# A two-layer graph kernel on one core: 13 adjacency tiles per chunk, four PSUM banks for the late chains, 41 split tiles, and a first tile in four pieces

## The chip, the cores and the metric

The kernel runs on one core of a Trainium2 chip. The metric is device time in microseconds, lower is better. Times of the profile are counted from the start of its span.

## The reference

```python
N = 8192                      # nodes; 128 channels
h = maximum(layernorm(x), 0)
r = where((adj < 0.5) & ~eye, adj, 1.0)
S = where((adj < 0.5) & ~eye, exp(-(1/r - 1/mu)**2 / (2*sigma**2)), 0)
x = x + S @ (h @ W0 + B0)                 # layer 0
h = maximum(layernorm(x), 0)
x = x + (adj*adj + eye) @ (h @ W1.T)      # layer 1
```

`adj` is 8192x8192 in fp32, 256 MB. Layer 0 needs a nonlinear function of each element, layer 1 its square.

## The kernel before

Everything is transposed: channels on partitions. `adj` is cut into 16x16 blocks of 512x512; a block is one tile of 128x2048 fp32 (1 MB, four groups of 128 columns of `adj`). Row block c of layer 0 ("chunk c", steps 16c to 16c+15) takes 16 S tiles. Step s masks S tile s; `square(s-2)` and `sensitivity(s-2)` run two steps behind, and TensorE multiplies S tile s-3 in step s.

**An S tile** passes through five instructions: VectorE `premask` (cutoff, L604), ScalarE `log` (L778), ScalarE `reciprocal` (L783), VectorE `square` (L611), ScalarE `sensitivity` (L788); then TensorE's `l1` (L434, four fp32 matmuls, eight records) into `p_l1a` or `p_l1b`. A diagonal block first gets 1 added to its diagonal (`add_eye`, L589), which the cutoff then masks out.

**An adj tile** of layer 1 is an `Item` (row, source): it is squared in place by VectorE (`square_adj`, L622) or ScalarE (L796), a diagonal one gets the eye added, and TensorE multiplies it with the second layer's features of the source block (L468). The features of a source block exist only once its chunk of layer 0 is done (`add_x1` L677, `relu_row` L684, `keep_h2` L691 on VectorE, `centre_row` L503 on TensorE, and so on). `make_plan` therefore fills chunk c with tiles whose source is known: `QUOTA[c]` tiles, and the rest comes in the last chunk (steps 240 to 255, "dense") and behind it (the "tail", one tile per step). Most tiles of a row form a `Chain`: consecutive tiles that sum in one PSUM bank. At the chain's end VectorE copies the bank to `xa_buf` (`add_chain`, L718), and GpSimd's queue adds the buffer onto the output in DRAM (L893). In steady chunks the chains use banks `p_x0` and `p_x1`; before, only the last 16 chains, those of the tail, use four (also `p_own0` and `p_l1a`).

**A split tile** is written as two fp32r tiles, `high` (a CAST, L639) and `low` (the difference, L641), by `halves` on VectorE; TensorE then makes three matmuls per group (L446 to L448, twelve records) in place of a group's two fp32 records. There are three `high` buffers, so `halves` of split tile n waits for TensorE to have used split tile n-3. On VectorE the halves of item m stand behind the squaring of item m+1.

All engines run their instructions in the order written. The loads of both kinds of tiles share a ring of 8 buffers (`A_RING`), S tiles one of 7, of which the dense chunk uses three: `premask(t)` there waits for `s_used`, TensorE's end of S tile t-3. `EVAC` is the number of items after a chain's last one at which VectorE copies its bank. SP's queue issues all loads in order.

## Time and profile before

| | us |
|---|---|
| median of 3 runs | 1880.04 |
| lowest, highest | 1878.95, 1880.99 |
| the profiled execution | 1879.75 |
| its span | 1877.9 |
| TensorE busy | 1840.0 |
| VectorE busy | 1723.2 |
| ScalarE busy | 1730.2 |

The busy times are sums of records, and a matmul's record lasts longer than the distance to the next one, so they hide gaps. The distance between two starts on an engine is called its pitch below. A chunk is measured from one `centre_row` to the next.

### The profile page before, as it was taken

What the parts mean: (1) busy time and instruction counts of PE and PEld (TensorE: products, weight loads), DVE (VectorE), ACT (ScalarE), POOL (GpSimd) and SP (SyncE); (2) the same over time, 40 slices, a digit from 0 to 9 for tenths busy, and PEclk for the clock granted to TensorE, in tenths of its full rate; (3) what the DMA queues carried; (4) which work ended last, traced back from release to release, by engine and by line L of the source; (5) the groups of instructions that cost most, each with busy time, mean ns of one, the idle gap of its engine ahead of it and who ended that gap; (6) DMA issues with size and microseconds to landing.
All of it is one profiled execution on the core that took longest, in us unless ns stands there. A gap on an engine that the chain in (4) does not pass through costs nothing.

```text
span 1877.9 us, 13284 instructions
## 1 busy us (share of the span) xinstructions
PE 1840.0 (98%) x4820; PEld 879.6 (47%) x4820; DVE 1723.2 (92%) x1012; ACT 1730.2 (92%) x986; POOL 87.6 (5%) x110
## 2 busy tenths in 40 slices
PE   7999999999999999999999999999999999999998
PEld 4544444444444444444444444444444444555565
DVE  7999999999999999999999999999999955678686
ACT  8999999999999999999999999999999997777562
POOL 0000000000000000000000000000000000000011
PEclk9999999999999999999999999999999999999999
DMA  8476878987878787777677776666666578667997
GB/s 312 163 292 260 326 281 305 323 294 285 307 269 324 235 297 258 251 275 257 245 253 266 258 286 239 242 219 229 220 227 218 191 265 287 248 251 259 309 353 226
DMA packets 83138, 497.85 MB, mean 265 GB/s; under 512 B 9601, under 2 KB 10241, under 8 KB 26881
## 3 DMA queue, kind: packets, MB, share of 16 engines
q1 hardware_dynamic: 68832, 469.33, 65.4%
q0 software_dynamic: 14096, 27.53, 8.4%
q8 instruction: 39, 0.64, 0.1%
q14 instruction: 27, 0.21, 0.0%
q10 hardware_dynamic: 144, 0.13, 0.0%
HBM read 469.17 MB, written 27.79 MB: 265 GB/s over the span
## 4 chain that ended last, share of the span: by engine, by line
PE 43%; ACT 32%; DVE 18%; issue 6%; DMA 1%; SPq 0%; DVEq 0%; ACTq 0%
PE p_x L468 12%; PE p_l1b L434 11%; ACT rings L778 10%; ACT rings L783 9%; ACT rings L788 9%; PE p_l1a L434 8%; PE p_own L468 7%; DVE rings L611 6%; DVE rings L604 6%; DVE rings L622 3%; ACT rings L796 2%; PE p_x L446 1%; PE p_x L448 1%; PE p_x L447 1%; DVE high L639 1%
## 5 line engine op out<-in xcount | busy, mean ns | idle before, releaser
L611 DVE SCALAR_TENSOR_TENSOR rings<-rings,small 128x2048 f32<-128x2048 f32 x256 | 600.5, 2346 | 29.0 <-ACT rings L783 28.8
L604 DVE SCALAR_TENSOR_TENSOR rings<-rings 128x2048 f32<-128x2048 f32 x256 | 585.1, 2286 | 8.2 <-PE p_l1b L434 6.8
L788 ACT ACTIVATE rings<-rings,small 128x2048 f32<-128x2048 f32 x256 | 533.0, 2082 | 34.3 <-DVE rings L611 33.9
L778 ACT ACTIVATE rings<-rings,small 128x2048 f32<-128x2048 f32 x256 | 509.4, 1990 | 9.3 <-DVE rings L604 6.8
L468 PE MATMUL p_x<-rings,h 128*128 128x512 f32 x1128 | 505.4, 592 | 0.0
L783 ACT ACTIVATE rings<-rings 128x2048 f32<-128x2048 f32 x256 | 488.0, 1906 | 5.5
L434 PE MATMUL p_l1b<-rings,h 128*128 128x512 f32 x1024 | 460.9, 596 | 3.6 <-ACT rings L788 3.5
L434 PE MATMUL p_l1a<-rings,h 128*128 128x512 f32 x1024 | 459.5, 595 | 0.2
L468 PEld LDWEIGHTS p_x<-rings,h 128*128 128x128 f32 x1128 | 213.5, 190 | 261.1 <-issue 260.0
L622 DVE TENSOR_TENSOR rings<-rings 128x2048 f32<-128x2048 f32 x135 | 308.5, 2285 | 7.3 <-DMA rings<-adjT 4.6
L434 PEld LDWEIGHTS p_l1b<-rings,h 128*128 128x128 f32 x1024 | 194.3, 191 | 245.4 <-issue 236.9
L434 PEld LDWEIGHTS p_l1a<-rings,h 128*128 128x128 f32 x1024 | 193.6, 191 | 237.1 <-issue 234.2
L796 ACT ACTIVATE rings<-rings 128x2048 f32<-128x2048 f32 x121 | 226.7, 1900 | 59.5 <-DMA rings<-adjT 31.3
L468 PE MATMUL p_own<-rings,h 128*128 128x512 f32 x600 | 269.7, 592 | 0.0
L468 PEld LDWEIGHTS p_own<-rings,h 128*128 128x128 f32 x600 | 113.6, 190 | 138.0 <-issue 137.3
L893 POOL DMA_DIRECT2D outT<-xa_buf x89 | 74.2, 834 | 1502.6 <-DVE xa_buf L718 1455.3
L718 DVE COPY xa_buf<-p_x 128x512 f32<-128x512 f32 x82 | 56.1, 684 | 57.6 <-PE p_x L468 48.0
L641 DVE TENSOR_TENSOR low<-rings,high 128x2048 fp32r<-128x2048 f32 x37 | 84.8, 2293 | 1.3
L639 DVE CAST high<-rings 128x2048 fp32r<-128x2048 f32 x37 | 45.2, 1222 | 13.4 <-ACT rings L796 13.3
L446 PE MATMUL p_x<-high,h_high 128*128 128x512 f32 x108 | 49.2, 456 | 5.4 <-DVE low L641 5.4
L448 PE MATMUL p_x<-high,h_low 128*128 128x512 f32 x108 | 42.2, 391 | 0.0
L447 PE MATMUL p_x<-low,h_high 128*128 128x512 f32 x108 | 42.2, 390 | 0.0
(92 smaller groups left out, 498.9 us busy)
## 6 DMA issues: line engine op xcount, KB each, us to landing
rings<-adjT SPq DMA_DIRECT2D x439, 1024.0 KB, 6.9
outT<-xa_buf POOLq DMA_DIRECT2D x89, 256.0 KB, 5.7
x_buf<-xT SPq DMA_DIRECT2D x24, 256.0 KB, 6.7
outT<-y_buf POOLq DMA_DIRECT2D x15, 256.0 KB, 5.9
xa_buf<-xT SPq DMA_DIRECT2D x8, 256.0 KB, 5.9
outT<-x_buf POOLq DMA_DIRECT2D x1, 256.0 KB, 4.8
y_buf<-outT SPq DMA_DIRECT2D x1, 256.0 KB, 13.1
outT<-y_buf SPq DMA_DIRECT2D x1, 128.0 KB, 1.7
```

Source lines behind the costliest of these rows:

```text
L434: last = pe.matmul(p_l1[c % 2][:, :], h1[:, J * G + g, :], block_of(s_ring, slot_of(t), g), start=(i == 0 and g == 0), stop=(i == NC - 1 a ...
L446: pe.matmul(out[:, :], h_high, high, start=(it.first and g == 0), stop=False)
L468: last = pe.matmul(out[:, :], h2[:, it.source * G + g, :], block_of(a_ring, it.load % A_RING, g), start=(it.first and g == 0), stop=(it.la ...
L604: dve.scalar_tensor_tensor(out=tile(s_ring, slot_of(t)), in0=tile(a_ring, slot), scalar=CUTOFF, in1=tile(a_ring, slot), op0=ALU.is_lt, op1 ...
L611: dve.scalar_tensor_tensor(out=v, in0=v, scalar=neg_2c, in1=v, op0=ALU.add, op1=ALU.mult).then_inc(squared, 1)
L622: squares = dve.tensor_tensor(a, a, a, ALU.mult)
L641: dve.tensor_tensor(low_ring[it.load % A_RING][:, :], squares, high[:, :].bitcast(F32), ALU.subtract).then_inc(low_ready, 1)
L778: act.activation(v, v, ACT.Ln, bias=tiny_c).then_inc(ln_done, 1)
L783: act.activation(v, v, ACT.Exp, scale=-1.0).then_inc(recip_done, 1)
L788: act.activation(v, v, ACT.Exp, bias=exp_bias, scale=neg_k).then_inc(sens_done, 1)
L796: act.activation(a, a, ACT.Square).then_inc(q_by["act"], 1)
L893: pool.dma_start(columns(outT, ch.row), xa_buf[ch.index % XA_RING][:, :], accum_op=how).then_inc(xa_stored[ch.index % XA_RING], 16)
```

## The change

`QUOTA` gives chunk 1 eleven tiles in place of ten, chunks 2 and 6 to 14 thirteen in place of twelve. The dense chunk keeps 45 tiles of 56. The tail has 34 tiles as before, but begins with chains of four tiles of row 12 and three of row 13. Chains that begin from step 246 on are `wide`: they use four banks, and are copied six items after their end, or two items before their bank is needed. There are 98 chains (90 before). 41 tiles are split (37 before), five of seven in the tail. Diagonal tiles from step 240 on (`late`) are squared by ScalarE, VectorE only adds the eye. In the dense chunk VectorE masks at the first item of a step, not the middle one; row 15's steps in the tail come one item later. The first tile is loaded by four DMAs of 128x512, behind the first block of x, and masked and given to the logarithm in four pieces.

```diff
--- before.py
+++ after.py
@@ -28,10 +28,12 @@
-QUOTA = [0, 10] + [12] * 13
+QUOTA = [0, 11, 13] + [12] * 3 + [13] * 9
 S_STEPS = NC * NC
 H2_STEP = 6
-TAIL = 3
+END_ROWS = [12, 13, 0, 1, 2, 3, 4, 5, 6, 7, 8, 9, 10, 11, 14, 15]
+KEPT = [(12, 12), (12, 13), (13, 13)]
 OPEN = 4
 LAST = S_STEPS - NC
@@ -45,6 +47,10 @@
 SPLIT_ORDER = list(SPLIT_STEP)
 EVAC = 3
 EVAC_STEPS = 3
+WIDE_STEP = 6
+EVAC_WIDE = 6
+AHEAD = 2
 STEAL = 0.5
@@ -68,8 +74,8 @@
     if c < NC - 1:
         n = QUOTA[c]
         return [(2 * k + 1) * NC // (2 * n) for k in range(n)]
-    n = NC * NC - 2 * NC + 1 - sum(QUOTA) - TAIL
-    return [(2 * k + 1) * NC // (2 * n) for k in range(n)] + [NC + k for k in range(TAIL)]
+    n = NC * NC - 2 * NC + 1 - sum(QUOTA) - len(KEPT)
+    return [(2 * k + 1) * NC // (2 * n) for k in range(n)]
 def next_chain(c, places, done):
@@ -90,7 +96,7 @@
 def make_plan():
-    done, chains, items, order = set(), [], [], [list(range(NC))]
+    done, chains, items, order = set(KEPT), [], [], [list(range(NC))]
     for c in range(1, NC):
         places = slots_of(c)
         own = [J for J in range(c) if (c, J) not in done][-len(places):]
@@ -126,14 +132,17 @@
                 if own_here:
                     picked.insert(here[len(here) // 2], picked.pop(own_here[0]))
         items += [Item(row, J, chain, c * NC + i) for i, row, J, chain in picked]
-    ends = [Chain(row, [J for J in range(NC) if (row, J) not in done], True) for row in range(NC)]
+    done -= set(KEPT)
+    ends = [Chain(row, [J for J in range(NC) if (row, J) not in done], True) for row in END_ROWS]
     chains += ends
-    tail = [(ch, ch.sources[0]) for ch in ends[:OPEN]] + [(ch, ch.sources[1]) for ch in ends[:OPEN]]
+    tail = [(ch, J) for ch in ends[:OPEN] for J in ch.sources[:-1]] + [(ch, ch.sources[-1]) for ch in ends[:OPEN]]
     tail += [(ch, J) for ch in ends[OPEN:] for J in ch.sources]
-    items += [Item(ch.row, J, ch, S_STEPS + TAIL + k) for k, (ch, J) in enumerate(tail)]
+    items += [Item(ch.row, J, ch, S_STEPS + k) for k, (ch, J) in enumerate(tail)]
     for k, ch in enumerate(chains):
         ch.index = k
-        ch.bank = (k - len(chains) + NC) % OPEN if ch.final else k % 2
+        begin = min(it.step for it in items if it.chain is ch)
+        ch.wide = begin >= LAST + WIDE_STEP
+        ch.bank = (k - len(chains) + NC) % OPEN if ch.wide else k % 2
     return chains, items, order
@@ -161,7 +170,7 @@
 SPLITS = [it for it in ITEMS if it.step >= LAST + SPLIT_STEP.get(it.source, STEPS) and it.row != it.source
-          and it.m % 5 % 2 == 0]
+          and it.m % 7 not in (1, 4)]
 for it in ITEMS:
     it.split = None
 for r, it in enumerate(SPLITS):
@@ -174,6 +183,7 @@
         it.by = "act"
     else:
         it.by = "act" if it.m % (5 if it.step < 4 * NC else 4) == 3 and it.row != it.source else "dve"
+    it.late = it.row == it.source and it.step >= S_STEPS - NC
     if it.row == it.source:
         it.by = "dve"
     Q_COUNT[it.by] += 1
@@ -186,6 +196,7 @@
 for it in ITEMS:
     peers = [x for x in ITEMS if x.chain is it.chain and x.row == it.row]
     it.first, it.last = it is peers[0], it is peers[-1]
+LATE = [it.m for it in ITEMS if it.late]
 OWN_LAST = {it.row: it.m for it in ITEMS if it.own and it.last}
 for ch in CHAINS:
     mine = [it for it in ITEMS if it.chain is ch]
@@ -213,7 +224,10 @@
         ch.evac = first_item(ch.end + EVAC_STEPS) - 0.5
         EVAC_AT.setdefault(ch.end + EVAC_STEPS, []).append(ch)
     else:
-        ch.evac = max(ch.last_m + EVAC, CHAINS[ch.index - 1].evac)
+        ch.evac = max(ch.last_m + (EVAC_WIDE if ch.wide else EVAC), CHAINS[ch.index - 1].evac)
+        if ch.wide:
+            ch.evac = min([ch.evac] + [o.first_m - AHEAD for o in CHAINS[ch.index + 1:] if o.bank == ch.bank])
         EVAC_AFTER.setdefault(min(ch.evac, len(ITEMS)), []).append(ch)
     TRANSFERS.append((ch.evac + 0.2, 0, ch.index))
@@ -385,10 +403,12 @@
                     sp.wait_ge(y_ready, c - 2)
                 sp.dma_start(x_buf[c % 2][:, :], columns(xT, c)).then_inc(x_loaded[c % 2], 16)
-            load_tile(0)
             load_nodes(0)
+            for g in range(G):
+                sp.dma_start(block_of(a_ring, 0, g),
+                             adjT[0, :, g * CHUNK:(g + 1) * CHUNK]).then_inc(first_loaded[g], 16)
+            load_tile(1)
             load_nodes(1)
-            load_tile(1)
             sp.dma_start(mu_c, mu.partition_broadcast(P)).then_inc(params_loaded, 16)
             sp.dma_start(sigma_c, sigma.partition_broadcast(P)).then_inc(params_loaded, 16)
             load_nodes(2)
@@ -452,12 +472,12 @@
                 if it.first and it.own:
                     if it.row >= 3:
                         pe.wait_ge(y_ready, it.row - 2)
-                elif it.first and it.chain.final and it.chain.bank == 2 and it.chain.row < OPEN:
-                    pe.wait_ge(y_ready, NC - 2)
-                elif it.first and it.chain.final and it.chain.bank == 3 and it.chain.row < OPEN:
-                    pe.wait_ge(x1_added, NC - 1)
                 elif it.first and it.chain.after:
                     pe.wait_ge(xa_added, it.chain.after[-1].index + 1)
+                elif it.first and it.chain.bank == 2:
+                    pe.wait_ge(y_ready, NC - 2)
+                elif it.first and it.chain.bank == 3:
+                    pe.wait_ge(x1_added, NC - 1)
                 if it.split is not None:
                     l2_split(it)
                     return
@@ -588,6 +608,17 @@
                 d = diagonal(ring, slot)
                 return dve.tensor_tensor(d, d, eye[:, :].unsqueeze(1).to_broadcast([P, G, P]), ALU.add)
+            def premask_first():
+                for g in range(G):
+                    dve.wait_ge(first_loaded[g], 16)
+                    v = block_of(a_ring, 0, g)
+                    marks = v[:, g * P:(g + 1) * P]
+                    dve.tensor_tensor(marks, marks, eye[:, :], ALU.add).then_inc(first_marked, 1)
+                    dve.wait_ge(first_marked, g + 1)
+                    piece = dve.scalar_tensor_tensor(out=block_of(s_ring, 0, g), in0=v, scalar=CUTOFF, in1=v,
+                                                     op0=ALU.is_lt, op1=ALU.mult)
+                    piece.then_inc(first_premasked if g < G - 1 else premasked, 1)
             def premask(t):
                 c, i = divmod(t, NC)
                 load = S_LOAD[t]
@@ -627,6 +658,10 @@
                     squares = add_eye(a_ring, slot)
                 squares.then_inc(q_by["dve"], 1)
+            def add_late_eye(it):
+                dve.wait_ge(late_squared, LATE.index(it.m) + 1)
+                add_eye(a_ring, it.load % A_RING).then_inc(q_by["dve"], 1)
             def halves(it):
                 squares = tile(a_ring, it.load % A_RING)
@@ -720,14 +755,14 @@
             def row_steps(c, i):
                 if c > NC:
                     return
-                fast = c < NC - 1
-                if i == 3:
+                fast, end = c < NC - 1, c == NC
+                if i == (4 if end else 3):
                     add_x1(c - 1)
-                if i == (4 if fast else 5):
+                if i == (4 if fast else 6 if end else 5):
                     relu_row(c - 1)
-                if i == 5 and c >= 2:
+                if i == (5 if end else 5) and c >= 2:
                     add_y(c - 1)
-                if i == (6 if fast else 7 if c == NC else 8):
+                if i == (6 if fast else 8 if end else 8):
                     keep_h2(c - 1)
                     if c == NC:
                         split_h2(NC - 1)
@@ -737,7 +772,9 @@
                 if 2 <= s < S_STEPS + 2:
                     square(s - 2)
                 dense = LAST <= s < S_STEPS
-                if s < S_STEPS and not dense:
+                if s == 0:
+                    premask_first()
+                elif s < S_STEPS and not dense:
                     premask(s)
                 if c >= 1:
                     row_steps(c, i)
@@ -747,15 +784,19 @@
                     if s < S_STEPS:
                         split_h2(J)
                 for it in AT_STEP[s]:
-                    if dense and it is AT_STEP[s][len(AT_STEP[s]) // 2]:
+                    if dense and it is AT_STEP[s][0]:
                         premask(s)
-                    if it.by == "dve":
+                    if it.by == "dve" and not it.late:
                         square_adj(it)
+                    if it.m and ITEMS[it.m - 1].late:
+                        add_late_eye(ITEMS[it.m - 1])
                     if it.m and ITEMS[it.m - 1].split is not None:
                         halves(ITEMS[it.m - 1])
                     for ch in EVAC_AFTER.get(it.m, []):
                         add_chain(ch)
                     if it.m == len(ITEMS) - 1:
+                        if it.late:
+                            add_late_eye(it)
                         if it.split is not None:
                             halves(it)
                         for ch in EVAC_AFTER.get(it.m + 1, []):
@@ -772,6 +813,16 @@
             act.preload_act_table_set("natural_log_exp_and_others")
             act.wait_ge(param_step, 3)
+            def log_first():
+                for g in range(G):
+                    if g < G - 1:
+                        act.wait_ge(first_premasked, g + 1)
+                    else:
+                        act.wait_ge(premasked, 1)
+                    v = block_of(s_ring, 0, g)
+                    piece = act.activation(v, v, ACT.Ln, bias=tiny_c)
+                piece.then_inc(ln_done, 1)
             def log(t):
                 act.wait_ge(premasked, t + 1)
                 v = tile(s_ring, slot_of(t))
@@ -793,7 +844,11 @@
                 if it.own:
                     act.wait_ge(premasked, LOADS[it.load][0] + 1)
                 a = tile(a_ring, slot)
-                act.activation(a, a, ACT.Square).then_inc(q_by["act"], 1)
+                squares = act.activation(a, a, ACT.Square)
+                if it.late:
+                    squares.then_inc(late_squared, 1)
+                else:
+                    squares.then_inc(q_by["act"], 1)
             def square_nodes(n):
                 act.wait_ge(node_relu, n + 1)
@@ -841,12 +896,14 @@
                 dense = LAST <= s < S_STEPS
                 if 2 <= s < S_STEPS + 2:
                     sensitivity(s - 2)
-                if s < S_STEPS and not dense:
+                if s == 0:
+                    log_first()
+                elif s < S_STEPS and not dense:
                     log(s)
                 if c >= 1:
                     row_steps(s)
                 for it in AT_STEP[s]:
-                    if it.by == "act":
+                    if it.by == "act" or it.late:
                         square_adj(it)
                 if dense:
                     log(s)
```

VectorE's order at the start. Before, the first tile is marked and masked whole:

```order
L589 TENSOR_TENSOR rings<-rings,eye 128x4x128
L604 SCALAR_TENSOR_TENSOR rings<-rings 128x2048
L658 TENSOR_SCALAR normed_buf<-p_stat 128x512
L604 SCALAR_TENSOR_TENSOR rings<-rings 128x2048
L658 TENSOR_SCALAR xa_buf<-p_x 128x512
```

and in the changed kernel in four quarters:

```order
L616 TENSOR_TENSOR rings<-rings,eye 128x128
L618 SCALAR_TENSOR_TENSOR rings<-rings 128x512
L616 TENSOR_TENSOR rings<-rings,eye 128x128
L618 SCALAR_TENSOR_TENSOR rings<-rings 128x512
L616 TENSOR_TENSOR rings<-rings,eye 128x128
L618 SCALAR_TENSOR_TENSOR rings<-rings 128x512
L616 TENSOR_TENSOR rings<-rings,eye 128x128
L618 SCALAR_TENSOR_TENSOR rings<-rings 128x512
L693 TENSOR_SCALAR normed_buf<-p_stat 128x512
L635 SCALAR_TENSOR_TENSOR rings<-rings 128x2048
L693 TENSOR_SCALAR xa_buf<-p_x 128x512
```

The first relu of x (L658, now L693) comes behind four marks and four masks. ScalarE's logarithm of this tile becomes four of 128x512, and its other instructions keep their order.

VectorE's order late in the dense chunk. Before, where a step begins with `square` (L611), the halves of the last item of the step ahead follow, and then the mask of this step (L604):

```order
L611 SCALAR_TENSOR_TENSOR rings<-rings,small 128x2048
L639 CAST high_58<-rings 128x2048
L641 TENSOR_TENSOR low_49<-rings,high_58 128x2048
L604 SCALAR_TENSOR_TENSOR rings<-rings 128x2048
L639 CAST high_59<-rings 128x2048
L641 TENSOR_TENSOR low_52<-rings,high_59 128x2048
L718 COPY xa_buf<-p_x 128x512
L611 SCALAR_TENSOR_TENSOR rings<-rings,small 128x2048
```

In the changed kernel, steps 253 and 254 (square L642, mask L635, halves L674 and L676, chain copy L753):

```order
L642 SCALAR_TENSOR_TENSOR rings<-rings,small 128x2048
L635 SCALAR_TENSOR_TENSOR rings<-rings 128x2048
L674 CAST high_57<-rings 128x2048
L676 TENSOR_TENSOR low_51<-rings,high_57 128x2048
L642 SCALAR_TENSOR_TENSOR rings<-rings,small 128x2048
L635 SCALAR_TENSOR_TENSOR rings<-rings 128x2048
L674 CAST high_58<-rings 128x2048
L676 TENSOR_TENSOR low_52<-rings,high_58 128x2048
```

The mask has moved ahead of the halves of the step before. The second mask here is mask 254, and the halves behind it are those of tile (15,13), the last item of step 253.

Behind the last S tile, VectorE's order at the four-tile chain of row 12 in the changed kernel, whose names show the buffers (the first pair are the halves of (13,15), the COPY empties that chain's bank, the second pair are the halves of (0,15)):

```order
L674 CAST high2_59<-rings 128x2048
L676 TENSOR_TENSOR low4_53<-rings,high2_59 128x2048
L753 COPY xa_buf2<-p_x0 128x512
L674 CAST high0_57<-rings 128x2048
L676 TENSOR_TENSOR low5_54<-rings,high0_57 128x2048
```

Before, no chain there is longer than two tiles, and this copy is that of a two-tile chain of row 0.

## Rows read from the trace of the kernel before

**Rows 1.** The page, busy time and share of the span: each engine, us and instructions

```profile
PE 1840.0 (98%) x4820; PEld 879.6 (47%) x4820; DVE 1723.2 (92%) x1012; ACT 1730.2 (92%) x986; POOL 87.6 (5%) x110
```

**Rows 2.** Windows: stretch, length, busy PE, PEld, DVE, ACT, POOL, clock, DMA share, GB/s

```profile
129.88:231.66 101.78, 98.70 (x235) 44.99 (x234) 101.04 (x58) 98.37 (x55) 5.22 (x9) 0.97 0.74 281
231.66:734.02 502.36, 496.19 (x1211) 222.56 (x1209) 496.94 (x266) 488.86 (x267) 27.96 (x35) 1.00 0.82 293
734.02:1428.22 694.20, 693.06 (x1694) 312.61 (x1695) 677.46 (x346) 689.14 (x379) 23.41 (x27) 1.00 0.69 246
832.90:931.68 98.78, 98.78 (x243) 44.74 (x243) 96.52 (x50) 98.40 (x55) 3.45 (x4) 1.00 0.72 255
...
1800.00:1850.00 50.00, 50.00 (x173) 32.21 (x172) 41.03 (x30) 28.73 (x15) 7.99 (x8) 1.00 1.04 369
```

**Rows 3.** Timeline of TensorE late in the dense chunk: start, length, line, operation

```profile
1742.50 3.60 PE L468 MATMUL p_x<-rings,h 128*128 128x512 f32 x8
...
1751.39 3.59 PE L468 MATMUL p_x<-rings,h 128*128 128x512 f32 x8
1754.82 3.60 PE L434 MATMUL p_l1b<-rings,h 128*128 128x512 f32 x8
```

**Rows 4.** Waits from 1557.9 us on: who for whom, us, times, longest

```profile
DVE xa_buf L718 <- PE p_x L468: 33.0, 6, 9.6
...
DVE xa_buf L718 <- PE p_x L448: 9.6, 4, 5.2
...
PE p_x L446 <- DVE low L641: 5.4, 6, 1.5
```

**Rows 5.** Timeline of VectorE and ScalarE in the first 20 us

```profile
6.41 2.29 DVE L604 SCALAR_TENSOR_TENSOR rings<-rings 128x2048 f32<-128x2048 f32 x1
...
8.80 2.00 ACT L778 ACTIVATE rings<-rings,small 128x2048 f32<-128x2048 f32 x1 [6.77 <-DVE rings L604]
...
9.89 2.29 DVE L604 SCALAR_TENSOR_TENSOR rings<-rings 128x2048 f32<-128x2048 f32 x1 [0.58 <-DMA rings<-adjT]
...
16.79 2.29 DVE L604 SCALAR_TENSOR_TENSOR rings<-rings 128x2048 f32<-128x2048 f32 x1 [0.20 <-DMA rings<-adjT]
...
19.55 1.99 ACT L778 ACTIVATE rings<-rings,small 128x2048 f32<-128x2048 f32 x1
```

**Rows 6.** Timeline of VectorE without gaps, for the pitches

```profile
1722.97 2.28 DVE L604 SCALAR_TENSOR_TENSOR rings<-rings 128x2048 f32<-128x2048 f32 x1
1725.17 1.22 DVE L639 CAST high<-rings 128x2048 fp32r<-128x2048 f32 x1
1726.42 2.29 DVE L641 TENSOR_TENSOR low<-rings,high 128x2048 fp32r<-128x2048 f32 x1
1728.63 2.28 DVE L622 TENSOR_TENSOR rings<-rings 128x2048 f32<-128x2048 f32 x1
...
1731.56 2.34 DVE L611 SCALAR_TENSOR_TENSOR rings<-rings,small 128x2048 f32<-128x2048 f32 x1
1733.82 0.68 DVE L718 COPY xa_buf<-p_x 128x512 f32<-128x512 f32 x1
1734.42 0.68 DVE L589 TENSOR_TENSOR rings<-rings,eye 128x512 f32<-128x512 f32 x1
```

**Rows 7.** Timeline of ScalarE: a logarithm, then reciprocal and sensitivity, then a square

```profile
1685.37 1.99 ACT L778 ACTIVATE rings<-rings,small 128x2048 f32<-128x2048 f32 x1
...
1691.20 1.90 ACT L796 ACTIVATE rings<-rings 128x2048 f32<-128x2048 f32 x1
```

**Rows 8.** The chain that ended last, near the end: start, length, what

```profile
1838.71 12.75 DMA rings<-adjT
1851.49 2.30 DVE rings L622
```

**Rows 9.** Timeline of ScalarE in the tail: squares that wait for loads

```profile
1794.44 1.91 ACT L796 ACTIVATE rings<-rings 128x2048 f32<-128x2048 f32 x1 [0.40 <-DMA rings<-adjT]
...
1845.27 1.91 ACT L796 ACTIVATE rings<-rings 128x2048 f32<-128x2048 f32 x1 [1.91 <-DMA rings<-adjT]
```

4 lines of the change are left out of this document (added).

## The prediction

> **What bounds the kernel now.** I read the page first: TensorE is busy 98% of the span, VectorE and ScalarE 92% [rows 1]. Three engines near their limit give no answer, so the next view is the table of windows, cut at the `centre_row` of each chunk. Chunk 8 is the cleanest: 98.78 us, PE busy in all of it at the full clock, VectorE 96.5, ScalarE 98.4 [rows 2]. The timeline gives the pitch, which matters more than the record's length, since matmul records overlap: an ordinary 128x2048 tile (eight half-passes) goes from 1751.39 to 1754.82, 3.43 us; one ordinary tile and two split ones take 1742.50 to 1751.39, so a split tile is (8.89 - 3.43)/2 = 2.73 us [rows 3]. Chunk 8 has 16 S tiles and 12 adj tiles: 28 x 3.43 = 96.0, plus 2.7 for centring, variance and projection, is 98.8: a chunk of 12 tiles at TensorE's own floor.
>
> So count what TensorE loses against that floor. Chunk 1 has 10 tiles, floor 98.78 - 2 x 3.43 = 91.9, and takes 101.78: 9.9 lost. Chunks 2 to 6 take 502.36 against 5 x 98.78 = 493.9: 8.5 lost. Chunks 7 to 13 take 694.20 against 691.5: 2.7 lost [rows 2]. In the lossy chunks VectorE is full (101.04 of 101.78; 496.9 of 502.4). In the dense last chunk and the tail TensorE waits for VectorE's `low` six times, 5.4 us; the records there run 0.16 past the pitch, so about 6.5 us is lost. VectorE itself stands still for 43 us before copies of finished chains (33.0 + 9.6) [rows 4]. In the first 20 us work is paced by loads and by ScalarE [rows 5].
>
> **The sum starts from this:** the number of tiles does not change (256 S, 256 adj). Where TensorE is at its floor, moving a tile from the last chunk to an earlier one moves 3.43 us and saves nothing. A gain can come only from lost time that shrinks, from tiles that become split, and from the start.
>
> **1. Thirteen-tile chunks.** VectorE's prices by pitch: mask 2.20 (1722.97 to 1725.17), CAST 1.25, `low` 2.21, square of a diagonal tile with its mark 2.93 (so a plain one, a record as long as the mask's, 2.2, and the mark 0.7), S square 2.26, copy 0.60 [rows 6]. ScalarE's logarithm, reciprocal and sensitivity take 5.83 together, its square of adj 1.9 [rows 7]. The plan gives:
> - Chunk 1: 11 tiles for 10, the added one squared on VectorE: VectorE +2.2, TensorE +3.43. VectorE binds, so the chunk grows by 2.2: 1.2 saved.
> - Chunks 2 to 6: 62 tiles for 60; VectorE squares 49 for 48, chain copies 35 for 30, diagonal tiles 4 for 3: 2.2 + 5 x 0.60 + 0.7 = 5.9 more. ScalarE gets one square more, 1.9. TensorE gets 6.9. If VectorE goes on binding, 6.9 - 5.9 = 1.0 saved.
> - Chunks 7 to 13: TensorE's floor becomes 98.78 + 3.43 = 102.2. VectorE needs 16 x (2.20 + 2.26) = 71.4, ten squares 22.0, the row's four steps and the mark 3.1, up to five copies 3.0 and two diagonal tiles 1.4: 101 at most; ScalarE 16 x 5.83 + 0.9 + four squares 7.6 = 101.8 in two chunks, 99.9 in the rest. TensorE alone binds, and of 2.7 lost I give 2.6 back.
> Together **-4.8 us**. Bounds: 0 if the small waits stay whatever the load; -9 if the longer TensorE chunks let the 7-slot S ring carry VectorE's lead over.
>
> **2. Four more split tiles** (41 for 37, 5 of 7 for 3 of 5): 4 x (3.43 - 2.73) = **-2.8 us** on TensorE. They cost VectorE 1.25 + 2.21 = 3.46 each. In the steady tail seven tiles are then 5 x 2.73 + 2 x 3.43 = 20.5 for TensorE and 5 x 3.46 + 3.5 copies x 0.60 = 19.4 for VectorE: cover remains, but 5% of it where there was 21% (five tiles: 15.0 against 11.9). Without cover a split tile is worth nothing.
>
> **3. Order in the dense chunk and the tail.** Chains that begin from step 246 on use four banks and are copied six items later. So VectorE no longer stands in front of a copy that TensorE has not finished, which is what makes `low` late now. Diagonal tiles are squared on ScalarE, which spares VectorE 2.2 and, at the end, its own wait for a load: now tile (14,14) lands 12.75 us after its issue, VectorE stands before it, and the split of the tile ahead is late [rows 8]. Against that stand two new places. Mask 254 stands ahead of the split of tile (15,13). It waits until TensorE has done S tile 251; behind that S tile stand tile (0,13) and then (15,13). TensorE arrives after 3.43 us; VectorE needs 0.1 + 2.20 + 3.46 = 5.8 us. That stalls TensorE 2.4 us. In the other dense steps with a split last item two tiles stand ahead (at least 6.2 us), which is just enough. The second: the four-tile chain of row 12 must leave its bank before chain 2 needs it, so its copy stands before the split of (0,15), two tiles behind TensorE: 0.1 + 0.60 + 3.46 = 4.1 against 2.73, 1.4 us, and about 0.6 for the tile before. Sum 4.4 in place of 6.5: **-2.1 us**. Bounds: -6.5 if none of the new waits shows, +3 if 5% of cover is not enough.
>
> **4. The start.** Now the first tile is masked from 6.41 to 8.70, and its logarithm runs from 8.80 to 10.80 [rows 5]. In pieces the last quarter lands at about 6.4, my estimate (the whole tile landed before its mark, some 0.7 ahead of the mask, and 256 KB of x are now ahead of it), then a mark of 0.3, a mask of about 0.7 and a logarithm of about 0.6 (the 128x512 rows): 8.0, so 2.8 us earlier. What follows does not move as far: logarithm 1 waits for a mask that started when its load landed (9.89), and mask 2 starts when load 2 lands (0.20 idle to 16.79); its logarithm could begin at 19.1 instead of 19.55. Against that the second block of x now stands behind tile 1 in the queue and so comes after 9.89, in front of TensorE's statistics. I take **-0.5 us**, bounds -2.8 and +1.2.
>
> A rule speaks against the pieces: the Trainium skill, "VectorE: DVE Perf Modes", on the TRN2 errata, says that small tiles pay a fixed latency each; its (N+151)/0.96 gives 4 x 691 = 2764 ns for four quarters against 2291 for one. This trace's 128x512 copy (0.68) and 128x2048 mask (2.29) agree. By that rule alone the start would be 0.5 us worse instead of 0.5 better; the sum would be 1 us higher.
>
> **5. The end** stays: the last tile (15,15) is not split in either; after it come two half adds and a store, as now. Chains 10, 11 and 14 are now copied after the last mark, but the first two while TensorE still works, the third before the last add where another copy stood: 0.
>
> **Sum** against the profiled execution's 1879.75 (span 1877.9): 4.8 + 2.8 + 2.1 + 0.5 = 10.2, so 1869.6. The median of the runs shown is 0.3 above; **1869.5** is my figure. What a measurement here can tell from no change is 0.2%, 3.8 us.
>
> **Rivals.**
> - *The lost time goes nearly altogether* (0.16). For it: chunks 7 to 13 show what happens where VectorE has 2% of slack, 0.4 us lost per chunk. With -9, -2.8, -6.5 and -1: 1860.5, its range 1857 to 1865.
> - *The tail runs into the loads* (0.15). At 1800 to 1850 the DMA engines are busy 1.04 of their time [rows 2], and ScalarE waits for nearly each landing: from 1794.44 to 1845.27 are 15 tiles at 3.39 us, where TensorE takes (2 x 3.43 + 3 x 2.73)/5 = 3.01 [rows 9]. Against it: the tail began with tiles squared far ahead, and only 0.4 to 0.5 us per tile of that is used up; the last load is issued before the margin ends. If it is, TensorE loses (3.39 - 2.93) on the last ten tiles, 4.6 us: 1874, and 1877 with VectorE's jitter.
> - *Only the splits pay* (0.10). The chunks lose the same 21 us because the waits belong to the lockstep of VectorE and ScalarE, and the tail's new waits eat the old ones: 1879.75 - 2.8 = 1877.
> - *VectorE becomes the bound of the 13-tile chunks* (0.06), slower. Chunks 2 to 6, with nine or ten squares and four to eight copies, average 100.5 [rows 2]; chunks 6 to 14 would need 102.2 plus (10.2 + 3.8)/9 = 1.6, so 103.8 each, before the kernel is slower by more than 0.2%. Chunk 6 gets eleven squares and two diagonals and may come near; the others have nine or ten, so I see no row that speaks for it. At 104.3 the time would be 1869.6 + 9 x 2.1 = 1888.
>
> **Chances.** Forecast 1865 to 1873: 0.53. Faster by over 0.2%: 0.53 + 0.16 + 0.15, 0.84; within: 0.10; slower: 0.06. The range of 8 in 10 is 1863 to 1877: above it lie the slower case and part of the two at 1877, below it half of the first rival.
>
> **What would show it.** Chunks 7 to 14 at 102.2 us each with PE without a gap; chunk 1 at about 104, chunks 2 to 6 together at about 508; split tiles still at 2.73; VectorE's waits before chain copies down from 43 us to under 10; one wait of 2 to 2.5 us at the split of (15,13) behind a mask that waited for PE; ScalarE's second logarithm about 1 us earlier, its third about 0.5. The prediction is wrong if 13-tile chunks come out over 103, if TensorE waits in the last 30 tiles for more than 4 us, or if the statistics of the first x blocks leave ScalarE's second logarithm later than now.

## The result, and the profile after

The changed kernel takes 1873.01 us, median of 6 executions (1871.82 to 1875.2), against 1879.94 (1878.95 to 1881.48) before: ratio 0.9963, interval 0.995 to 0.9976. That is 6.9 us faster, inside the predicted range and 3.5 above the predicted 1869.5. The profiled execution took 1873.83 with a span of 1872.0, 5.9 less than the span before. The account below is of the two spans.

The page of the changed kernel, busy time per engine:

```profile
PE 1836.9 (98%) x4836; PEld 886.5 (47%) x4836; DVE 1744.1 (93%) x1035; ACT 1732.5 (93%) x988; POOL 95.7 (5%) x118
```

TensorE loses 3.1 us of busy time and VectorE gains 20.9. The windows, cut where each chunk's `centre_row` begins (chunk 1, chunks 2 to 5, chunks 6 to 13, then one steady chunk; columns as in [rows 2]):

```profile
131.78:241.40 109.62, 106.02 (x251) 47.93 (x250) 108.88 (x61) 103.00 (x57) 6.31 (x11) 0.97 0.76 284
241.40:645.72 404.32, 399.75 (x977) 180.02 (x976) 401.45 (x219) 392.71 (x215) 26.87 (x33) 1.00 0.85 297
645.72:1463.42 817.70, 817.70 (x2001) 369.98 (x2000) 794.31 (x409) 795.82 (x435) 31.09 (x36) 1.00 0.73 257
...
952.36:1054.57 102.21, 102.21 (x251) 46.25 (x250) 99.47 (x52) 100.83 (x56) 4.31 (x5) 1.00 0.79 272
```

The third row is the change's best part: eight chunks of thirteen tiles in 817.70 us, PE busy in all of it, 102.21 each, the predicted floor. In the second row TensorE still stands still for 4.6 us. Chunk 1 is full on VectorE, 108.88 of 109.62, and yet it is not VectorE that costs its time. TensorE has one stand there, for ScalarE's squares in the row's variance, which come behind a sensitivity and a logarithm on ScalarE (133.82 to 137.70 before). Before, and in the changed kernel:

```profile
138.33 1.86 PE L509 MATMUL p_stat<-mean_of,square_buf 128*128 128x1 f32 x8 [3.08 <-ACT square_buf L816]
```

```profile
140.93 1.77 PE L529 MATMUL p_stat<-mean_of,square_buf 128*128 128x1 f32 x8 [3.60 <-ACT square_buf L871]
```

Beside it come 6.8 us at a granted clock of 0.50 (the column before the DMA share; full speed, 1.00, is the 2.4 GHz level and half the 1.2 GHz one), and then the rest of the chunk without a gap. First before, then the changed kernel:

```profile
137.80:144.60 6.80, 6.27 (x14) 3.69 (x15) 6.76 (x5) 6.77 (x7) 0.00 (x0) 0.50 0.43 157
```

```profile
141.10:147.90 6.80, 6.80 (x15) 3.70 (x16) 6.76 (x5) 6.77 (x6) 0.00 (x0) 0.50 0.42 157
147.90:241.40 93.50, 93.50 (x219) 41.38 (x218) 93.47 (x53) 86.94 (x46) 6.31 (x11) 1.00 0.80 296
```

The stand and half of the slow stretch outside it are 6.2 us before and 7.0 now. That is nearly all that chunk 1 loses (6.4 and 7.4, counted as below). All fourteen profiles have this stand (3.1 or 3.6 us) and this stretch.

The waits of the dense chunk and the tail (from 1557.9 us), who for whom, us, times, longest:

```profile
DVE rings L635 <- PE p_l1b L454: 31.0, 12, 7.9
...
DVE xa_buf L753 <- PE p_x L488: 13.0, 3, 10.9
...
PE p_own L466 <- DVE low L676: 3.6, 2, 2.6
...
DVE xa_buf L753 <- PE p_own L468: 2.9, 1, 2.9
...
PE p_x L466 <- DVE low L676: 0.5, 1, 0.5
```

Two lines of the same view of before, which rows 4 leave out:

```profile
DVE rings L604 <- PE p_l1b L434: 6.8, 2, 5.4
...
PE p_own L446 <- DVE low L641: 0.6, 1, 0.6
```

VectorE's waits before copies of bank `p_x` fell from 43 us to 13 (before copies of `p_own` from 6.5 to 2.9), but its masks (L635) now wait 31.0 us for TensorE, in place of 6.8. TensorE waits for `low` three times in place of seven, 4.1 us in place of 6.0; the prediction had counted six and 5.4. One of the three is that of tile (15,13). VectorE there, then TensorE:

```profile
1717.75 2.29 DVE L635 SCALAR_TENSOR_TENSOR rings<-rings 128x2048 f32<-128x2048 f32 x1 [4.43 <-PE p_l1b L454]
1719.96 1.22 DVE L674 CAST high<-rings 128x2048 fp32r<-128x2048 f32 x1
1721.21 2.29 DVE L676 TENSOR_TENSOR low<-rings,high 128x2048 fp32r<-128x2048 f32 x1
```

```profile
1723.65 0.47 PE L466 MATMUL p_own<-high,h_high 128*128 128x512 f32 x1 [2.58 <-DVE low L676]
...
1725.30 0.63 PE L466 MATMUL p_own<-high,h_high 128*128 128x512 f32 x1
...
1727.86 1.23 PE L454 MATMUL p_l1b<-rings,h 128*128 128x512 f32 x2
```

Mask 254 stands before the halves of (15,13) and had stood 4.43 us for TensorE. Then mask, CAST and `low` run without a gap, and TensorE idles 2.58 for the last of them. This is the wait that the prediction named, with 2.4. What it did not name follows: from 1724.87 on the records are 0.63 long and 0.43 apart, where full speed has 0.39 and 0.23. Windows of the same stretch show the granted clock at half:

```profile
1718.00:1723.60 5.60, 3.07 (x8) 1.04 (x6) 5.57 (x4) 3.79 (x3) 0.00 (x0) 1.00 0.43 183
...
1724.90:1727.80 2.90, 2.90 (x8) 2.27 (x7) 2.90 (x3) 2.76 (x2) 0.00 (x0) 0.50 0.00 0
1728.00:1731.00 3.00, 3.00 (x8) 1.33 (x7) 2.97 (x3) 0.00 (x0) 0.83 (x1) 0.96 0.53 183
```

Seven matmuls 0.20 further apart each are 1.4 us on top of the idle. The other two waits stand at the chain of row 12, the tile before it and (0,15), as forecast:

```profile
1787.02 0.47 PE L466 MATMUL p_x<-high,h_high 128*128 128x512 f32 x1 [0.48 <-DVE low L676]
...
1791.08 0.47 PE L466 MATMUL p_own<-high,h_high 128*128 128x512 f32 x1 [1.05 <-DVE low L676]
```

The start, on VectorE, ScalarE and TensorE:

```profile
5.23 0.29 DVE L616 TENSOR_TENSOR rings<-rings,eye 128x128 f32<-128x128 f32 x1 [3.30 <-DMA rings<-adjT]
...
7.79 0.29 DVE L616 TENSOR_TENSOR rings<-rings,eye 128x128 f32<-128x128 f32 x1 [1.54 <-DMA rings<-adjT]
...
9.98 0.69 DVE L618 SCALAR_TENSOR_TENSOR rings<-rings 128x512 f32<-128x512 f32 x1
10.71 0.72 ACT L823 ACTIVATE rings<-rings,small 128x512 f32<-128x512 f32 x1 [0.21 <-DVE rings L618]
11.64 2.29 DVE L635 SCALAR_TENSOR_TENSOR rings<-rings 128x2048 f32<-128x2048 f32 x1 [0.38 <-DMA rings<-adjT]
12.30 2.08 PE L496 MATMUL p_x<-x_buf,centre_w 128*128 128x512 f32 x2 [6.46 <-DMA x_buf<-xT]
13.97 2.00 ACT L829 ACTIVATE rings<-rings,small 128x2048 f32<-128x2048 f32 x1 [0.26 <-DVE rings L635]
...
21.14 2.00 ACT L829 ACTIVATE rings<-rings,small 128x2048 f32<-128x2048 f32 x1
```

The first quarter is there early, but the fourth is masked only at 9.98, so the first tile's logarithm ends at 11.43; whole, it ended at 10.80 [rows 5]. Tile 1 is masked at 11.64 (9.89 before), the third logarithm begins at 21.14 (19.55 before), and TensorE's second centring (12.30) had waited 6.46 us for x. The second logarithm begins at 13.97. Before, it was here:

```profile
12.99 1.99 ACT L778 ACTIVATE rings<-rings,small 128x2048 f32<-128x2048 f32 x1
```

The prediction had it about 1 us earlier, and named a later one as a sign of being wrong; it is 1.0 later.

**The account.** "Lost" is TensorE's time over 3.43 us per ordinary tile, 2.73 per split tile and 2.7 per row's steps, each chunk's tiles counted by its matmul records. (So counted, the window of chunk 1 held eleven tiles before, not ten, and holds thirteen now; before, its loss was 6.4 us, not 9.9.)

| part | before | after | difference | predicted |
|---|---|---|---|---|
| `centre_row` 0 begins | 129.9 | 131.8 | +1.9 | -0.5 |
| lost in chunks 1 to 13 | 17.7 | 13.2 | -4.5 | -4.8 |
| four more split tiles | | | -2.8 | -2.8 |
| lost in the dense chunk and tail | 8.0 | 7.0 | -1.0 | -2.1 |
| last matmul to the end of the span | 6.9 | 7.4 | +0.5 | 0 |
| sum | | | -5.9 | -10.2 |

The second row of the table hides a spread. Chunk 1 loses 1.0 more than before (the prediction had it lose 1.2 less), chunks 2 to 6 lose 5.8 for 8.5, 2.7 less (1.0 was predicted), and chunks 7 to 13 lose nothing for 2.7 (2.6 was predicted).

So the experiments have three questions: what the start costs and why, whether the mask's place is the tail's loss, and what the table of chunk sizes is worth by itself. The ratios are to the kernel before, measured beside each group (1880.16 for s1 to s3 and c1, 1880.14 for a0, t1, t2 and d1, 1879.88 for the rest).

### The profile page after: what moved, and what is told of

It is laid out like the page before. It is cut to its first block, busy times and chain, and to the rows that moved or that the text cites. A ratio compares the mean times of both kernels' runs of the same rounds, so it can differ in the third digit from the quotient of the medians.

```text
span 1872.0 us, 13372 instructions
## 1 busy us (share of the span) xinstructions
PE 1836.9 (98%) x4836; PEld 886.5 (47%) x4836; DVE 1744.1 (93%) x1035; ACT 1732.5 (93%) x988; POOL 95.7 (5%) x118
## 4 chain that ended last, share of the span: by engine, by line
PE 77%; DVE 11%; ACT 8%; issue 3%; DMA 0%; SPq 0%; DVEq 0%
PE p_x L488 21%; PE p_l1b L454 20%; PE p_l1a L454 15%; PE p_own L488 11%; DVE rings L642 4%; DVE rings L635 3%; ACT rings L829 2%; DVE rings L653 2%; ACT rings L834 2%; ACT rings L839 2%; PE p_l1a L488 1%; PE p_x L466 1%; PE p_x L468 1%; PE p_x L467 1%; PE p_own L466 1%
## 5 line engine op out<-in xcount | busy, mean ns | idle before, releaser
L635 DVE SCALAR_TENSOR_TENSOR rings<-rings 128x2048 f32<-128x2048 f32 x255 | 582.5, 2284 | 35.3 <-PE p_l1b L454 31.0
L642 DVE SCALAR_TENSOR_TENSOR rings<-rings,small 128x2048 f32<-128x2048 f32 x256 | 600.1, 2344 | 14.4 <-ACT rings L834 14.2
L488 PE MATMUL p_x<-rings,h 128*128 128x512 f32 x1144 | 513.3, 592 | 0.0
L488 PE MATMUL p_own<-rings,h 128*128 128x512 f32 x520 | 233.6, 592 | 0.0
L488 PEld LDWEIGHTS p_own<-rings,h 128*128 128x128 f32 x520 | 98.4, 190 | 120.1 <-issue 119.6
L950 POOL DMA_DIRECT2D outT<-xa_buf x97 | 82.1, 849 | 1422.7 <-DVE xa_buf L753 1410.1
L676 DVE TENSOR_TENSOR low<-rings,high 128x2048 fp32r<-128x2048 f32 x41 | 94.0, 2292 | 1.4
L753 DVE COPY xa_buf<-p_x 128x512 f32<-128x512 f32 x86 | 58.6, 682 | 16.9 <-PE p_x L488 16.9
L674 DVE CAST high<-rings 128x2048 fp32r<-128x2048 f32 x41 | 50.0, 1220 | 13.3 <-ACT rings L847 13.3
L466 PE MATMUL p_x<-high,h_high 128*128 128x512 f32 x92 | 41.5, 451 | 0.5 <-DVE low L676 0.5
L468 PE MATMUL p_x<-high,h_low 128*128 128x512 f32 x92 | 35.9, 391 | 0.0
L467 PE MATMUL p_x<-low,h_high 128*128 128x512 f32 x92 | 35.9, 390 | 0.0
```

What stands on the lines that cost most here:

```text
L466: pe.matmul(out[:, :], h_high, high, start=(it.first and g == 0), stop=False)
L488: last = pe.matmul(out[:, :], h2[:, it.source * G + g, :], block_of(a_ring, it.load % A_RING, g), start=(it.first and g == 0), stop=(it.la ...
L635: dve.scalar_tensor_tensor(out=tile(s_ring, slot_of(t)), in0=tile(a_ring, slot), scalar=CUTOFF, in1=tile(a_ring, slot), op0=ALU.is_lt, op1 ...
L642: dve.scalar_tensor_tensor(out=v, in0=v, scalar=neg_2c, in1=v, op0=ALU.add, op1=ALU.mult).then_inc(squared, 1)
L676: dve.tensor_tensor(low_ring[it.load % A_RING][:, :], squares, high[:, :].bitcast(F32), ALU.subtract).then_inc(low_ready, 1)
L950: pool.dma_start(columns(outT, ch.row), xa_buf[ch.index % XA_RING][:, :], accum_op=how).then_inc(xa_stored[ch.index % XA_RING], 16)
```

## Experiments: the start

**s1, the start of before** in the changed kernel:

```diff
+            load_tile(0)
             load_nodes(0)
-            for g in range(G):
-                sp.dma_start(block_of(a_ring, 0, g),
-                             adjT[0, :, g * CHUNK:(g + 1) * CHUNK]).then_inc(first_loaded[g], 16)
-            load_tile(1)
             load_nodes(1)
+            load_tile(1)
...
-                if s == 0:
-                    premask_first()
-                elif s < S_STEPS and not dense:
+                if s < S_STEPS and not dense:
                     premask(s)
```

(and the same for the logarithm).

> The changed kernel with the start as before: one load of the first tile, loads in the old order, one mask and one logarithm. My theory now: the new start costs about 1.9 us, since the first centre_row begins at 131.8 against 129.9 us in the kernel before. Then this run begins it at 129.9 to 130.2 and takes 1871.1 (1.9 below the changed kernel's 1873.0). Rival (the prediction's term): the pieces save 0.5 us and the later centre_row comes from chunk 1's eleventh tile; then 1873.5, centre_row still at about 131.8.

Measured: 1871.55 us (1870.77 to 1872.2), ratio 0.9952 (0.9937 to 0.9966); span 1869.0; `centre_row` 0 at 130.1 and `centre_row` 1 at 238.7, where the changed kernel has 131.8 and 241.4.

**s2, quarters, but in the order of before:** the four quarter loads first, then x block 0.

```diff
-            load_nodes(0)
             for g in range(G):
                 sp.dma_start(block_of(a_ring, 0, g),
                              adjT[0, :, g * CHUNK:(g + 1) * CHUNK]).then_inc(first_loaded[g], 16)
-            load_tile(1)
+            load_nodes(0)
             load_nodes(1)
+            load_tile(1)
```

> The changed kernel with the four quarter loads first, then both blocks of x, then tile 1, so only the old order is back, the pieces stay. If the order costs it (the second block of x behind tile 1, TensorE's second centring at 12.3 against 8.2 us), most of the 1.9 us comes back: 1871.3, centring before 9.5 us. If the small transfers cost it (2 KB rows move slower than 8 KB rows), less than 0.7 us comes back: 1872.5.

Measured: 1871.28 us, 0.9953 (0.9936 to 0.9969), span 1869.8, `centre_row` 1 at 239.4.

**s3, the new order, but one load of the first tile,** masked and logged in quarters still:

```diff
-            for g in range(G):
-                sp.dma_start(block_of(a_ring, 0, g),
-                             adjT[0, :, g * CHUNK:(g + 1) * CHUNK]).then_inc(first_loaded[g], 16)
+            load_tile(0)
             load_tile(1)
```

> The changed kernel with one load of the first tile in the changed order (x, tile 0, tile 1, x), masked and given to the logarithm in four pieces once all of it is there. If the small transfers are the cost: tile 1's mask starts before 10.5 us (11.64 in the changed kernel), 1871.5. If the order is the cost: the second centring stays behind tile 1, at 10.5 to 12, and the time stays within 0.7 us of 1873.0.

Measured: 1871.25 us, 0.9951 (0.9936 to 0.9966), span 1870.0, `centre_row` 1 at 239.4. The timelines, s2 and then s3 (mark, second centring, mask of tile 1):

```profile
7.71 0.29 DVE L616 TENSOR_TENSOR rings<-rings,eye 128x128 f32<-128x128 f32 x1 [0.55 <-DMA rings<-adjT]
...
11.32 1.91 PE L496 MATMUL p_x<-x_buf,centre_w 128*128 128x512 f32 x2
...
12.78 2.29 DVE L635 SCALAR_TENSOR_TENSOR rings<-rings 128x2048 f32<-128x2048 f32 x1 [0.52 <-DMA rings<-adjT]
```

```profile
6.18 0.29 DVE L615 TENSOR_TENSOR rings<-rings,eye 128x128 f32<-128x128 f32 x1 [4.25 <-DMA rings<-adjT]
...
9.43 2.07 PE L494 MATMUL p_x<-x_buf,centre_w 128*128 128x512 f32 x2 [3.74 <-DMA x_buf<-xT]
...
10.50 2.28 DVE L634 SCALAR_TENSOR_TENSOR rings<-rings 128x2048 f32<-128x2048 f32 x1
```

and the second centring with one load in the old order, s1:

```profile
8.20 1.91 PE L491 MATMUL p_x<-x_buf,centre_w 128*128 128x512 f32 x2
```

s2 had been expected to centre before 9.5 us if the order were the cost; it centres at 11.32. Side by side (us; landings by the traces' landing events):

| | s1: one load, old order | s3: one load, new order | s2: pieces, old order | changed: pieces, new order |
|---|---|---|---|---|
| first tile all landed | 5.57 | 6.09 | 7.69 | 9.10 |
| tile 1 landed | 9.37 | 8.60 | 12.76 | 11.62 |
| x block 1 landed | 6.88 | 9.38 | 10.29 | 12.25 |
| second centring | 8.20 | 9.43 | 11.32 | 12.30 |
| `centre_row` 1 | 238.7 | 239.4 | 239.4 | 241.4 |
| median | 1871.55 | 1871.25 | 1871.28 | 1873.01 |

In either order the pieces bring tile 1 some 3.0 to 3.4 us later and the second centring 2.9 to 3.1. The new order alone moves the centring by 1.0 to 1.2, and brings tile 1 0.8 to 1.1 earlier. So most of the early delay is that of the pieces.

What of it reaches the end? The changed start appears in five profiles with this table of chunks, whose `centre_row` 1 comes at 240.4 to 241.4, 240.9 on average; the old start in four (s1, c1, b1, b2) at 238.5 to 239.6, 238.9 on average. The start costs about 2.0 us, 1.5 by the medians of s1. Either half undone brings back all of it within this spread of 1 us, so the halves do not add. By what path is open: s2's tile 1 lands later than that of the changed kernel, and s2 is faster. A view of the transfers in the first 9 us, the changed kernel and then s1 (last two columns, share and GB/s):

```profile
0.00:9.00 9.00, 2.04 (x2) 0.50 (x2) 2.84 (x10) 2.16 (x3) 0.49 (x5) 1.00 0.72 224
```

```profile
0.00:9.00 9.00, 2.63 (x3) 1.18 (x4) 3.99 (x8) 1.50 (x2) 0.49 (x5) 1.00 0.77 293
```

It is 224 GB/s against 293, with the DMA engines busy nearly as long. Two things change together in the pieces: the rows are a quarter as long, and there are three loads more to issue (that of tile 1 goes out at 3.08 us, at 1.65 in s3). No run here parts the two.

## Experiments: the tail

**a0, the changed kernel again,** beside t1, t2 and d1:

> The changed kernel unaltered, for a comparison on one chip with the three below. 1873 us; last matmul to end of span 7.4 us; the mask of step 254 again holds the split of (15,13), and TensorE loses about 2.6 us there and 1.3 us behind it.

Measured: 1872.61 us (1871.83 to 1873.99), 0.9962 (0.995 to 0.9975), span 1872.2, every part of the account within 0.2.

**t1, the dense chunk's mask in the middle of the step's tiles:**

```diff
                 for it in AT_STEP[s]:
-                    if dense and it is AT_STEP[s][0]:
+                    if dense and it is AT_STEP[s][len(AT_STEP[s]) // 2]:
                         premask(s)
```

> The changed kernel with the mask of the dense chunk back at the middle item of each step. My theory: the wait at (15,13) vanishes, with the stretch of slow matmuls behind it, and no other comes, since the late chain copies no longer stop VectorE: time lost between the centre_row of row 14 and that of row 15 falls from 4.8 to about 1 us, and the kernel takes 1869.3. Rival: ScalarE, whose squares of the own tiles wait for the mask, gets it later, and TensorE waits in other steps as it does in the kernel before (5.1 us lost there); then 1873.

Measured: 1869.54 us (1867.83 to 1869.76), 0.9943 (0.9931 to 0.9956), 3.1 less than a0. Its waits from 1586 us on:

```profile
DVE rings L635 <- PE p_l1b L454: 17.1, 5, 7.9
...
PE p_own L466 <- DVE low L676: 2.1, 2, 1.1
```

The wait of 2.58 is gone, and with it the half clock: in chunk 14 (between `centre_row` 14 and 15) the loss falls from 4.8 to 1.9. A wait of 2.6 us and the slow stretch behind it were worth 3.

**t2, 37 split tiles,** by the rule of before:

```diff
-          and it.m % 7 not in (1, 4)]
+          and it.m % 5 % 2 == 0]
```

> The changed kernel with the old rule for split tiles, 37 of them. My theory: each of the four fewer costs TensorE 0.70 us, 2.8 in all, but with three of five split the rule also leaves the tail's new waits shorter (2.3 us lost now), and (15,13) may no longer be split; so 1873 + 2.8 less up to 3: between 1873 and 1876. Rival, the prediction's term alone: 1875.8. A time at or below 1873 says that the four more splits bring nothing.

Measured: 1875.67 us (1873.53 to 1876.75), 0.9975 (0.9966 to 0.9984), 3.1 more than a0. Splits give back 2.8 by count. The loss around them moves too (2.0 more in chunk 14, 1.4 less behind it, 1.0 less in chunk 1), so the sum agrees more closely than its parts. Chunk 1 has no split tile: its loss is 6.4 or 7.4 from run to run with the same code (b2 and b1). In chunk 14 the stand at (15,13) grew from 2.58 to 3.29 us. That fits the prediction's sum for it, since here the tile ahead, (0,13), is split and covers 0.70 less; half the clock follows it too.

## Experiments: the chunks

**c1, the table of chunk sizes alone,** in the kernel of before:

```diff
-QUOTA = [0, 10] + [12] * 13
+QUOTA = [0, 11, 13] + [12] * 3 + [13] * 9
```

> The kernel before with the new table of tiles per chunk and nothing else. My theory: chunks 6 to 13 run at 102.2 us without a gap, and of the 21.1 us lost in chunks 1 to 13 about 4.5 us comes back: 1875.5. Dense chunk and tail keep their waits. Rival: the waits only move into the dense chunk, which now has as many splits on fewer tiles; then the gain is under 1.5 us: 1878.5 or more.

Measured: 1873.01 us (1872.22 to 1874.92), 0.9961 (0.9946 to 0.9976), where 1875.5 was expected: the full change's gain from one line. But the parts differ. Chunks 1 to 13 lose 13.1 (17.7 before, so -4.6), one tile more is split (-0.7), the dense chunk and tail lose 11.0 (+3.0; TensorE waits 7.4 us for `low`, and a stand of 2.28 at 1696.7 is followed by 3.4 us at half the clock). The rest is at the two ends: `centre_row` 0 0.9 earlier, and the end 3.2 shorter. The chain that ended last, in the changed kernel:

```profile
1865.30 0.42 DVE y_buf L745
1865.73 0.33 DVEq L241
```

and in c1:

```profile
1868.41 0.42 DVE y_buf L710
1868.84 0.33 DVEq L227
```

From the last piece of the chain (1866.06) to the end of the span (1872.0) are 5.9 us, in c1 (1869.17 to 1871.4) 2.2. In between lies GpSimd's drain at the end of the program, by its records in the trace 8.5 us long before and 4.9 in c1. So 3.2 us of c1's 7.1 belong to the end, and nothing in the edit accounts for them.

**d1, two small GpSimd transfers more** in the changed kernel (early, at places 20 and 21 of its list, into columns that nobody reads, with a wait for both at place 40), to see whether their number decides the drain:

```diff
+                if turn in (20, 21):
+                    pool.dma_start(small[:, 14 + turn % 2:15 + turn % 2],
+                                   mu.partition_broadcast(P)).then_inc(spare_loaded, 16)
```

> The changed kernel with two tiny loads more on the GpSimd queue, at about a fifth of the way, so that it issues 115 transfers as the kernel before with the new table does, and not 113. That kernel ends 3.7 us after its last matmul, the others 6.9 to 7.4, because GpSimd's drain at the end takes 4.9 us there and 8.5 to 9.0 here. If the number of transfers decides the drain, this run ends 3.7 us after its last matmul, 1869.4. If what decides is how the last stores follow each other, it stays at 7.4 and 1873.

Measured: 1872.06 us (1871.07 to 1873.47), 0.9958 (0.9945 to 0.997); the drain's record is 8.1 us, and from the last matmul to the end are 6.5 us. c1 and d1 have 115 transfers each, so their number alone does not decide it. c1 is the only one of the fourteen profiles with a short one.

**c2, everything but the table:**

```diff
-QUOTA = [0, 11, 13] + [12] * 3 + [13] * 9
+QUOTA = [0, 10] + [12] * 13
```

> The changed kernel with the old table of tiles per chunk (10, then 12 each). The last chunk then has 56 tiles again, and the new split rule finds 45 tiles in place of 41. Chunks 1 to 13 should lose 21 us again (16.6 in the changed kernel), the start costs its 2 us, eight more splits than before save 5.6: 1880.1 + 2 - 5.6 = 1876.5, if the dense chunk's waits stay as they are, with VectorE's cover thinner perhaps 1879. If the table is not what saves (rival: the kernel before with the table alone gained by its shorter drain), it comes to 1873 or below.

Measured: 1871.93 us (1871.59 to 1873.35), 0.9959 (0.9946 to 0.9971). I had expected 1876.5: a clear miss. Its windows, one early and eight steady chunks:

```profile
634.85:735.17 100.32, 99.27 (x243) 44.48 (x242) 98.29 (x53) 99.19 (x55) 4.32 (x5) 1.00 0.79 278
634.85:1429.45 794.60, 792.34 (x1937) 356.88 (x1937) 775.62 (x398) 788.32 (x433) 27.76 (x32) 1.00 0.70 250
```

and its waits from 1557 us on:

```profile
DVE rings L635 <- PE p_l1b L454: 28.5, 7, 7.1
...
PE p_own L466 <- DVE low L676: 1.6, 2, 1.1
PE p_x L466 <- DVE low L676: 1.6, 2, 1.1
```

The chunks lose what they lost before (17.8), so the table does bring its 4.5. But with the old table the last chunk is fuller: 45 tiles come to be split for 41 (2.8 us), and the wait of 2.58 is not there, since step 253 now ends with a tile that is not split, (4,12) (chunk 14 loses 2.4 for 4.8). Together 5.2, more than the table brings.

**q1, thirteen-tile chunks from 6 on,** with ten, rather than eleven and thirteen, ahead:

```diff
-QUOTA = [0, 11, 13] + [12] * 3 + [13] * 9
+QUOTA = [0, 10, 12] + [12] * 3 + [13] * 9
```

> The changed kernel with ten tiles in chunk 1 and twelve in chunk 2, as before, and thirteen in 6 to 14. My theory: in chunks 1 and 2 VectorE binds, so the two tiles cost 2.2 + 2.2 us and some copies there and 6.9 us in the last chunk, where TensorE binds: 1.0 to 2 us slower, 1874. Rival: the chunks 1 to 4, which lost more in the changed kernel than before (13.1 against 11.2 us), are better with fewer tiles: 1872 or below.

Measured: 1871.73 us (1871.14 to 1872.4), 0.9957 (0.9944 to 0.9971), where 1874 was expected. Chunks 1 to 5 and the first steps of 6 lose 15.0 for 13.2, so 1.8 of the table's gain is gone, with the same 41 split tiles. (The rival's reason holds in half: chunks 1 to 4 lose 1.2 less, but 5 and 6 lose 3.1 more.) But here step 253 has three tiles, so two stand ahead of its split last one, (11,13), the wait of 2.58 is not there, and chunk 14 loses 2.2. Its start is 1.4 earlier as well, which I cannot explain.

## Experiments: together

**b1, s1 and t1 together.**

> The changed kernel with the start of the kernel before and the mask of the dense chunk at the middle item. If the two costs are independent (start 1.6 to 2.2 us, mask 3.1 us): 1872.6 - 1.8 - 3.1 = 1867.7. If an earlier start only makes VectorE and ScalarE wait elsewhere: 1869.5, as with the mask alone.

Measured: 1868.09 us (1866.73 to 1868.7), 0.9936 (0.9924 to 0.9949). Expected was 1867.7. That agrees with two independent costs; the other expectation, 1869.5, lies outside the runs. Against the kernel before, b1 gains 1.2 us more than t1, and the intervals of the two ratios overlap.

**b2, b1 with the copy of the row-12 chain one item later:**

```diff
-AHEAD = 2
+AHEAD = 1
```

> The same, and the copy of a late chain's bank at the latest one item, not two, before the bank is needed, so that the copy of the four-tile chain of row 12 no longer stands in front of the split of (0,15). My theory: TensorE's 1.3 us at (0,15) vanishes, nothing else moves: 1866.4. Rival: the copy comes too late for chain 2, whose first tile then waits: 1867.7 or more.

Measured: 1867.24 us (1865.87 to 1868.89), 0.9934 (0.9921 to 0.9946); 1866.4 was expected. The timeline of TensorE shows the waits left there, 0.46 for the 1.05 at (0,15):

```profile
1781.38 0.47 PE L461 MATMUL p_x<-high,h_high 128*128 128x512 f32 x1 [0.46 <-DVE low L671]
...
1784.84 0.47 PE L461 MATMUL p_own<-high,h_high 128*128 128x512 f32 x1 [0.46 <-DVE low L671]
```

The loss behind `centre_row` 15 falls from 2.22 to 1.58. That the time follows (0.85 in the medians, with ranges that overlap) is likely, not shown. b2 is the best version: 12.6 us less than the kernel before, where the change as made has 6.9.

## Why the prediction was right, and where it was wrong

- **Thirteen-tile chunks**, -4.8 forecast: -4.5, and -4.6 in c1, but the parts were not those of the forecast. Right is chunks 7 to 13: TensorE binds them at 102.21 each, and no wait shows. Wrong is chunk 1. "VectorE binds, so the chunk grows by 2.2" took a full VectorE for the cause of the loss; the loss was one stand and the half clock beside it, both still there, so the added tiles cost TensorE their whole time (109.62 us where about 104 was the sign; the window also holds one tile more than was counted). That chunks 2 to 6 gave 2.7 for 1.0 made up for it: luck. "VectorE becomes the bound of the 13-tile chunks" did not happen.
- **Four more split tiles**, -2.8: right (t2, 3.1 in time).
- **Order in the dense chunk and the tail**, -2.1: right in its mechanism, too low in one size. Forecast were 2.4 us at (15,13) and 1.4 and 0.6 at the chain of row 12; idle were 2.58, 1.05 and 0.48. The sum of new waits was therefore right to 0.3. Missing is the half clock behind the first wait, 1.4 us. The loss before was also larger than its 6.5, 8.0 by the account: the waits for `low` were 6.0 and not 5.4, and the rest is not attributed. t1 takes the wait and the half clock away and gains 3.1. VectorE's waits did not go, as was said, but moved: from the copies to the masks.
- **The start**, -0.5 with a bound of +1.2: wrong in sign, +1.9 here and 1.5 to 2.0 by the runs together. The step that failed is "in pieces the last quarter lands at about 6.4": it landed at 9.10 and was marked at 9.66, behind the mask of the quarter ahead. I had counted 256 KB more ahead of it and no cost for the pieces. The same cost moved tile 1 (11.62 for 9.87), which the prediction left where it was. That x block 1 comes later was seen; the centring came 4.1 us later than with the old start (8.20 in s1), of which the order makes 1.0 to 1.2 and the pieces the rest. The Trainium skill's rule ("VectorE: DVE Perf Modes", on the TRN2 errata: small tiles pay a fixed latency each) points the right way, and the single records agree with it (0.69 and 2.29). Its sum, four pieces of 691 ns against 2291, explains 0.5 us of about 2, and s3, which keeps the small pieces on VectorE, takes the same time as s1.
- **The end**, 0: +0.5. Not tested by itself; the profiles with the same table of chunks and the same tail lie between 7.0 and 7.6, d1's at 6.5.
- **Rivals.** "The tail runs into the loads": no; TensorE waits for nothing in the last 25 tiles. "The lost time goes nearly altogether": in chunks 6 to 13 yes, in the rest no. "Only the splits pay": no.

What the prediction lacked altogether is that the parts are coupled by the plan. Each took its term against before with the other parts' effects fixed; c2 and q1 show that the table also decides how many tiles are split and which of them stands behind a mask that waits. The time lay inside the range, but of 10.2 us forecast between the spans 5.9 came: the start, the tail and the end all fell short, and in the chunks two errors offset each other. Open stay why GpSimd's drain was short in c1, and why `centre_row` 0 comes up to 1.4 us apart in kernels with the same start code (131.8 in the changed kernel, 131.0 in t1, 130.4 in q1).

## What to carry to other kernels

An instruction that must wait for the other engine, put ahead of what that engine will need next, can make that engine wait in its turn; look where the fewest tiles stand between the two, and move the waiting instruction one place back (here 3 of 1873 us, by one index). Cutting the first transfer into pieces helps only if the pieces arrive as fast as the whole; count also what they do to every load behind them, here 3 us. An engine that is busy all through a window need not be what the window loses time to: look first for single stands of the engine that binds, and at its clock. A planner's table is not worth the sum of the chunks it fills: count also what it leaves for the other rules to do.
